# Attention without softmax on one core: eight identity products of 256 columns become four of 512, a copy and a fold

## What is computed

```python
q = q * cos + _rotate_half(q) * sin        # k likewise
k = jnp.repeat(k, rep, axis=1)             # 8 heads become 16
v = jnp.repeat(v, rep, axis=1)
qp = _softmax_kernel(q, rand_matrix)       # normalised, projected to 8, then [sin, cos] / 4
kp = _softmax_kernel(k, rand_matrix)
kv = jnp.einsum('bhsf,bhsd->bsfd', kp, v)
out = jnp.einsum('bhsf,bsfd->bhsd', qp, kv)
```

## Time and profile before

| | |
|---|---|
| time, three runs | median 1851.57 us (1850.24 to 1861.25) |
| profiled execution | 1867.35 us, of which its span 1865.6 us |
| share of the span busy | PE 87%, PEld 67%, DVE 74%, ACT 55%, POOL 36% |
| TensorE's mean granted clock | 0.936 of 2.4 GHz |
| groups of sums on TensorE (L790) | first at 94.05 us, last ends at about 337.5 us |

### The profile page before, as it was taken

How to read it: one execution, slowest core, us unless ns; L and a number is a source line. 1 busy time by engine, 2 the same in 40 slices (tenths; PEclk the granted TensorE clock), 3 DMA queues, 4 the chain that set the end, 5 groups by cost and what they waited for, 6 DMA issues and landing times. The chain is left out here.

```text
span 1865.6 us, 34560 instructions
## 1 busy us (share of the span) xinstructions
PE 1618.1 (87%) x9650; PEld 1253.5 (67%) x9650; DVE 1373.3 (74%) x3710; ACT 1032.9 (55%) x2457; POOL 672.2 (36%) x842
## 2 busy tenths in 40 slices
PE   6897787679983776999999999997889999988997
PEld 5786676569982554554555555544789999967775
DVE  6778999256667887999888888832666666657777
ACT  2555465246664761466576767664556666643443
POOL 2545588410007633121236767620000000056662
PEclk9898899889995996899999999998999999999998
DMA  9322456654444887242354546414964444355552
GB/s 345 120 69 68 96 134 183 173 162 131 132 123 138 275 298 210 58 110 62 70 125 134 175 135 176 129 40 133 274 186 133 131 132 132 119 158 170 164 167 77
DMA packets 291879, 272.72 MB, mean 146 GB/s; under 512 B 138153, under 2 KB 260714, under 8 KB 289644
## 3 DMA queue, kind: packets, MB, share of 16 engines
q1 hardware_dynamic: 267960, 215.41, 39.9%
q0 software_dynamic: 18432, 50.36, 8.9%
q10 hardware_dynamic: 5332, 4.96, 0.8%
HBM read 136.84 MB, written 133.69 MB: 145 GB/s over the span
## 5 line engine op out<-in xcount | busy, mean ns | idle before, releaser
L1880 ACT ACTIVATE ca_PT<-ca_psS 128x512 f32<-128x512 f32 (+3 forms) x768 | 336.4, 494 | 206.0 <-PE ca_psS L1917 201.0
L1421 POOL DMA_INDIRECT g_y<-ys_scratch,pos x128 | 125.0, 977 | 434.7 <-POOLq L73 363.7
L1796 DVE CUSTOM_DVE_ANT_0 ca_masked_row<-ca_psM,mask_row 128x384 f32<-128x384 f32 (+3 forms) x512 | 224.2, 485 | 44.8 <-PE ca_psM L1900 42.7
L1917 PE MATMUL ca_psS<-ca_QS,ca_KS 128*128 128x512 f32 (+1 forms) x480 | 175.4, 369 | 1.4 <-ACT ca_PT L1880 1.4
L1800 DVE TENSOR_REDUCE ca_part<-ca_psM 128x1 f32<-128x512 f32 x256 | 163.6, 684 | 17.0 <-PE ca_psM L1900 15.6
L1929 PE MATMUL ca_psO<-ca_PT,ca_VA 128*17 128x512 f32 (+3 forms) x1536 | 163.1, 497 | 6.0 <-ACT ca_OT L1872 6.0
L790 PE MATMUL fa_psO<-fa_weighed,ident 128*128 128x256 f32 x512 | 132.0, 416 | 38.1 <-DVE fa_weighed L585 38.1
L1900 PE MATMUL ca_psM<-ca_KS,ca_QS 126*128 126x512 f32 (+2 forms) x480 | 159.5, 380 | 5.5 <-DVE ca_part L1796 4.3
L1917 PEld LDWEIGHTS ca_psS<-ca_QS,ca_KS 128*128 128x128 f32 x480 | 90.8, 190 | 87.4 <-ACT ca_PT L1880 58.5
L790 PEld LDWEIGHTS fa_psO<-fa_weighed,ident 128*128 128x128 f32 x512 | 104.9, 210 | 59.8 <-DVE fa_weighed L585 44.4
L391 POOL DMA_INDIRECT xs_scratch<-x_sb,pos x128 | 124.6, 973 | 55.9 <-ACT ca_PT L1880 34.2
(11 more groups left out here) (271 smaller groups left out, 4656.1 us busy)
## 6 DMA issues: line engine op xcount, KB each, us to landing
xs_scratch<-fa_blank SPq DMA_DIRECT2D x32, 640.0 KB, 4.9
x_sb<-xs_scratch SPq DMA_DIRECT2D x143, 128.0 KB, 2.1
ys_scratch<-x_sb SPq DMA_DIRECT2D x143, 128.0 KB, 1.7
xs_scratch<-fa_blank SPq DMA_DIRECT2D x32, 384.0 KB, 6.7
spare<-qk_scratch SPq DMA_DIRECT2D x24, 512.0 KB, 7.4
ca_QS<-qk_scratch SPq DMA_DIRECT2D x20, 512.0 KB, 6.2
ca_KS<-qk_scratch SPq DMA_DIRECT2D x20, 512.0 KB, 7.8
x_sb<-in_ffn SPq DMA_DIRECT2D x16, 608.0 KB, 4.1
```

Of the source, the lines that this page charges most:

```text
L1421: pool.indirect_dma_start(y[:, t % R, k, :], None, y_dram, bass.IndirectOffsetOnAxis(pos[:, t, k:k + 1], 0)).then_inc(got[t % R], 16)
L1796: ins = dve.tensor_tensor_reduce(masked_row[:, (n * NU + u) % BANKS, h * w:(h + 1) * w], bank[:, h * w:(h + 1) * w], mask_row[:, CHUNK - w ...
L1880: act.activation(PT[:, s % PTS, h, off:CHUNK], psS[(GH * s + h) % BANKS][:, off:CHUNK], ACT.Exp)\
L1917: pe.matmul(psS[tile % BANKS][:, off:CHUNK], KS[slot][:, h, kt * P:(kt + 1) * P], QS[slot][:, h, c * CHUNK + off:(c + 1) * CHUNK], start=T ...
```

## The change

`sum_groups` adds the eight groups in four products of 512 columns, two groups side by side; the two halves of the bank then hold the sums of the even and the odd groups. ScalarE copies the upper half to SBUF (`take_half`, a stage of lag 13), and TensorE adds that copy to the lower half by one more identity product (`fold`, lag 13, in the list ahead of `sum_groups`). `take_out` waits for the fold and moves to lag 14, the store to lag 15. To make room for the buffer `half`, `rot_a` and `rot_b` get one buffer in place of two, and GpSimd's `rotate` waits for the addition of the tile before.

```diff
-        qk, rot_a, rot_b, rot, sq, rotT = (sb(x, [P, 2, NQK]) for x in ("qk", "rot_a", "rot_b", "rot", "sq", "rotT"))
+        qk, rot, sq, rotT = (sb(x, [P, 2, NQK]) for x in ("qk", "rot", "sq", "rotT"))
+        rot_a, rot_b = sb("rot_a", [P, NQK]), sb("rot_b", [P, NQK])
...
-        out = sb("out", [P, 2, NQ])
+        out, half = sb("out", [P, 2, NQ]), sb("half", [P, 2, NQ])
...
-            in_steps(sp, (9, empty_late), (14, store), first=BESIDE, beside=beside)
+            in_steps(sp, (9, empty_late), (15, store), first=BESIDE, beside=beside)
...
+            def take_half(t, i, b):
+                act.wait_ge(sums_done, t + 1)
+                if late(t, 2):
+                    act.wait_ge(folded, t - 1)
+                act.activation(half[:, i % 2, :], psO[i % 2][:, NQ:2 * NQ], ACT.Copy).then_inc(half_out, 1)
+
             def take_out(t, i, b):
-                act.wait_ge(sums_done, t + 1)
+                act.wait_ge(folded, t + 1)
...
-            in_steps(act, (2, take_qkv), (10, sines), (3, keep_rotT), (13, take_out), (10, squares), (4, keep_p),
+            in_steps(act, (2, take_qkv), (10, sines), (3, keep_rotT), (14, take_out), (13, take_half), (10, squares), (4, keep_p),
                      (4, norm), first=BESIDE, beside=beside)
...
+                if t >= 1:
+                    pool.wait_ge(rot_done, t)
...
-                for g in range(KV_HEADS):
-                    ins = pe.matmul(psO[i % 2][:, 0:NQ], ident[:], weighed[:, i % 2, g, :], start=g == 0, stop=g == KV_HEADS - 1)
+                for g in range(0, KV_HEADS, 2):
+                    ins = pe.matmul(psO[i % 2][:, :], ident[:], weighed[:, i % 2, g:g + 2, :].rearrange("p g n -> p (g n)"),
+                                    start=g == 0, stop=g == KV_HEADS - 2, skip_group_check=True)
                 ins.then_inc(sums_done, 1)
+
+            def fold(t, i, b):
+                pe.wait_ge(half_out, t + 1)
+                pe.matmul(psO[i % 2][:, 0:NQ], ident[:], half[:, i % 2, :], start=False, stop=True, skip_group_check=True)\
+                  .then_inc(folded, 1)
             pe.wait_ge(ident_in, 16)
-            for n in range(TILES + 12):
+            for n in range(TILES + 13):
...
-                for lag, stage in ((3, transpose_rotated), (12, sum_groups), (4, random_projection)):
+                for lag, stage in ((3, transpose_rotated), (13, fold), (12, sum_groups), (4, random_projection)):
```

More of the change, by code:

```diff
@@ L429, in first_attention @@
          v_out, bias_part, rot_parts, rot_done, sq_done, n2_done, norm_done, norm_part, inv_done, rotT_done, rotT_out, p_done, p_out,
-         turns_part, turns_done, apart_done, sine_done, sines_done, A_done, centred, weighed_done, sums_done, out_done, ones_done) = (
+         turns_part, turns_done, apart_done, sine_done, sines_done, A_done, centred, weighed_done, sums_done, half_out, folded, out_done, ones_done) = (
             sem(x) for x in (
@@ L434, in first_attention @@
                 "norm_part", "inv_done", "rotT_done", "rotT_out", "p_done", "p_out", "turns_part", "turns_done", "apart_done", "sine_done",
-                "sines_done", "A_done", "centred", "weighed_done", "sums_done", "out_done", "ones_done"))
+                "sines_done", "A_done", "centred", "weighed_done", "sums_done", "half_out", "folded", "out_done", "ones_done"))
         x_in = [sem(f"x_in{g}") for g in range(QUADS)]
@@ L704, in rotate @@
                     pool.wait_ge(rotT_done, t - 1)
-                q3, a3, b3 = (x[:, i % 2, :].rearrange("p (h d) -> p h d", d=D) for x in (qk, rot_a, rot_b))
+                if t >= 1:
+                    pool.wait_ge(rot_done, t)
+                q3, a3, b3 = (x.rearrange("p (h d) -> p h d", d=D) for x in (qk[:, i % 2, :], rot_a[:, :], rot_b[:, :]))
                 cos_i = cos[:, i, :].unsqueeze(1).broadcast_to([P, QK_HEADS, D])
@@ L714, in rotate @@
                 pool.wait_ge(rot_parts, t * 3 + 3)
-                pool.tensor_tensor(rot[:, i % 2, :], rot_a[:, i % 2, :], rot_b[:, i % 2, :], ALU.add).then_inc(rot_done, 1)
+                pool.tensor_tensor(rot[:, i % 2, :], rot_a[:, :], rot_b[:, :], ALU.add).then_inc(rot_done, 1)
             pool.memset(ones[:].bitcast(F32), 1.0).then_inc(ones_done, 1)
```

## The result

The changed kernel takes 1922.43 us (median of 4 runs, 1918.04 to 1939.92), the kernel before 1852.62 (4 runs): ratio 1.0366, interval 1.0328 to 1.0404, some 68 us slower by the ratio. I had forecast 1883 and a range up to 1908. All ratios here are of executions in the faster of two states; one execution of the last experiment's twelve took 3006.93 us and is left out of its ratio. The profiled execution took 1918.04 us with a span of 1916.3, that of before 1867.35 with 1865.6, which is 15 us above its own median; so the two traces differ by 50.7 us only, and I compare them inside the stage. Outside it the trace of before is the longer one: its first sums start at 94.05 us and not at 87.83, and from the last copy to the end it takes 6.9 us more.

What follows compares the result with a forecast made beforehand. TensorE bounds the first attention to 150.47 us, then VectorE. Losses of 7.0 + 2 + 15.5 + 5 + 2.0 = 31.5 us, against the median of 1851.57, give 1883 us, +1.7%; range 1865 to 1908.

Steps and rivals of the forecast that it cites:

- the ring: VectorE-bound steps: TensorE and ScalarE wait for each other in one turn, 9.3 us a tile against VectorE's 7.4.
- Part 1: Sums on TensorE: four products of 512 columns for eight of 256 give 0, at worst -0.25 us a tile.
- The rival that a product is paid by the piece: Sums: a 512-column record costs the 0.216 us of a 256-column one, sums 1.72 us less, 1852 us; 3%.
- Parts 2 and 3: TensorE-bound steps: fold product 0.43 us a tile; with the wait for ScalarE's copy, sums start 1.7 us later.
- sum A: Five TensorE-bound steps with a fold, steps 13 to 17: 4 x 1.7 + 0.2 = 7.0 us lost.
- Part 4: VectorE-bound steps: a turn of 8.97 us plus 0.35 for table loads; ten steps cost 1.9 us each, 19 us.
- the clock term: Ten VectorE-bound steps: two groups of sums at the lower clock are no longer covered, +5 us.
- sum B: Six steps between 150.47 and 212.28 us, where VectorE also carries the routing: 2 us, 0 and 5 as ends.
- rival 3: TensorE's clock falls more often behind idle pauses; each further slow turn costs some 5 us, four give 1903 us; 20%.
- The tail: Last tiles, all in series: copies and folds before and behind the last sums, +2.0 us.
- C: Ten steps from 212.28 to 286.33 us: 19 us less 3.5 of cover by the `weighed` buffers, 15.5 us.
- Rival 1: ScalarE's copy is hidden, VectorE stays the bound; five folds of 0.43 and 2.0 at the end: 1856 us; 7%.

Runs made afterwards that it cites:

- the last experiment: Kernel before, with random_projection ahead of sum_groups in TensorE's list: 1852.47 us against 1857.99, ratio 0.9979.
- the copies first: Changed kernel, with `take_out` and `take_half` ahead of take_qkv in ScalarE's list: 1862.17 us against 1860.29 for the kernel before, ratio 1.0007.
- the wait alone: Kernel before, with only a wait added: sum_groups also waits for keep_rotT of the same step; 1891.09 us against 1860.35, ratio 1.0166.
- the wide products alone: Kernel before, with four products of 512 columns for the eight, no copy or fold, odd groups left out: 1855.86 us against 1859.29, ratio 1.0002.
- the narrow ones with the fold: Changed kernel, with eight products of 256 columns again, copy and fold kept: 1929.09 us, ratio 1.0374 to the kernel before.
- the shorter filling: Changed kernel, with two more unread products of 512 columns on TensorE ahead of the fold in steps 24 to 33: 1915.88 us, ratio 1.0289.
- the longer filling: Changed kernel, with two unread products of 512 columns ahead of the fold from step 18 on, not 24: 1903.29 us, ratio 1.0279.

## Why the prediction was wrong

**The direction and the ring were right, the size was not.** A ring of TensorE and ScalarE takes VectorE's place, and it is the order of two lists that closes it: shown by the copies first (ratio 1.0007 with all the work left in) and by the wait alone (1.0166 with none added).

**Part 1, the products: right.** 3.43 us for eight records, 3.45 for sixteen before. The rival that a product is paid by the piece is refuted by the wide products alone and by the narrow ones with the fold. One fp32 product is two records, and each record takes the time of two passes of its columns (0.216 us for 256, against 0.12 for 274 in a single pass), so four in all. Of the two rules of the Trainium skill, "TensorE: Matmul & The Clock Gate", section "Back-to-back issue gap", the traces here bear out N/2.4 + 2.5 ns and not the cheaper wide product.

**Parts 2 and 3: right in size, one step short.** The step of the TensorE-bound stretch grew from 8.55 to 10.37 us, by 1.8, where I had 1.7. The semaphore, which I put at 0.05 with no row behind it, is 0.06 (the copy ends at 258.37, the fold starts at 258.43). The five steps of sum A gave 7.4 us together, for 7.0. But the stretch measured 11.6: the fold of tile 5 falls in step 18, which I had given to VectorE, and TensorE waited 4.6 us in front of it, 4.2 us more for that step. The size varies with how many of these groups are slow: in the traces of the narrow products and of the shorter filling, which up to there differ from the changed kernel in nothing that bears on it, the stretch took 66.0 and 72.4 us, for 68.1.

**Part 4, the ring: right.** 8.97 us by terms, 9.05 measured with the clock held up. A turn with table loads took 1.77 us more, not 1.42: the other load delays the next copy `qk` too (2.06 us from the projection at 264.43, not 1.69). Over ten tiles, nearly all at the higher clock, the stretch took 93.7 us against 74.05, +19.7. I had 19, less 3.5 of cover, of which the trace shows little. That 19 and 19.7 are so near is partly luck: one turn of the ten was slow (10.74 us), and the last has no projection and took 7.07.

**The step that failed is the clock term.** I put 5 us, for two slow groups in ten steps, as many as before. In the changed kernel all sixteen groups of sums from tile 6 to tile 21 were slow. Filling the pause takes 111.9 - 93.7 = 18.2 us off tiles 12 to 22, and in the trace of the longer filling 70.3 - 61.5 = 8.8 off tiles 6 to 12: 27 us for the term of 5, and sum B (2) was in truth a clock term too. These are single traces, and the 8.8 is from an execution 16 us faster than its median; by the ratios the two fillings gave back 14 and 16 us, and the difference is open. My rival 3 had this mechanism, at 20%, but with the wrong numbers: it had four slow turns of 5 us, and there were sixteen, of some 1.8 us each in tiles 12 to 22 (18.2/10), and in the turn shown above the clock was down for only a part of it. I argued there from single groups behind single pauses, and did not ask what happens when every turn has a pause of 2.4 us or more.

**The tail** grew by some 6 us, not 2. In one step near the end, where both tables are loaded, the sums follow at 10.15 us, where the kernel before has 5.76. ScalarE's copy for the fold stands behind both loads there (349.38 and 350.97), and those behind the random projection and the sums; TensorE waits 4.93 us:

```profile
353.92 1.22 PE L805 MATMUL fa_psO<-fa_half,ident 128*128 128x256 f32 x2 [4.93 <-ACT fa_half L678]
```

In the sum of the prediction the stage grew by 31.5 us, in the two traces by 63.8: 11.6 for 7.0 (A), 8.5 for 2 (B), 37.9 for 20.5 (C and clock), 5.8 for 2.0 (tail).

**Rival 1** (the copy is hidden) names what the copies first achieve; in the change it didn't hold, for the reason given.

## What to carry to other kernels

Before adding a handshake between two in-order engines, add up the full turn: all that each does from one handshake to the next, in the order of the lists. If that is longer than the bound's time a tile, cheap work becomes the bound, and the place of an instruction in its list is worth more than its duration; put consumers of last step's results ahead of what waits for this step's. And price a pause on TensorE that comes back every turn with the sums behind it at the lower clock: in tiles 12 to 22 it cost about as much again (18.2 us) as the ring itself (19.7).

## What the runs showed of the hardware

In all sixteen turns of tiles 6 to 21, with pauses of 2.35 to 4.61 us ahead of the fold, the sums were slow. In the turn shown above the granted clock was 0.50 (1.2 GHz) from the fold on and 0.97 from 261.20 on, inside the sums. Over tiles 12 to 22 it was 0.80 of 2.4 GHz, a mix of 1.2 and 2.4. 1.7 us of products whose result nobody reads, in that pause, brought it to 0.98 and made the kernel faster. Pauses of 1.42 and 1.85 us, each turn, gave a mix of slow and fast turns (clock 0.88 and 0.83 over tiles 12 to 22). In the variant with the copies first TensorE also idles there, in shorter pieces (1.18 us at most), and its clock was 1.00. What decides between the two levels at 1.4 to 1.9 us is left open.
